# An expert gate with fewer steps and operands in PSUM, a transpose placed inside a product, and another order of work in the first, second and last pair

## What is computed

```python
y = einsum('bct,bcd->bdt', x, weights[condition])      # 64x64 per batch, one of 16
result = einsum('bnd,od->bno', y, W_base) + b_base     # 1024 -> 1024
logits = einsum('bnd,ed->bne', y, W_gate)              # 8 experts
top_p, top_i = top_k(softmax(logits), 2)
route_w = sum(one_hot(top_i) * top_p / sum(top_p))     # two experts have a weight
h  = einsum('bnd,erd->bner', y, A)                     # 8 experts x rank 16
hw = h * route_w
out = x + result + einsum('bner,eor->bno', hw, B)
```

## Time and profile before

| what | us |
|---|---|
| median of 3 runs (1004.4 to 1005.06) | 1004.57 |
| the profiled execution, whole | 1005.73 |
| its span (first to last instruction) | 1003.9 |
| TensorE matmuls busy in the span | 957.7 |
| VectorE busy | 612.8 |
| GpSimd busy | 536.2 |
| ScalarE busy | 385.5 |

### The profile page before, as it was taken

The page is one execution under the profiler, slowest core; times in us unless marked ns, Lnnn a source line. Parts: engine busy times, 40 slices in busy tenths (PEclk is TensorE's granted clock), DMA queues, the critical chain, the costliest instruction groups (busy, mean ns, idle before and its releaser), DMA issues.

```text
span 1003.9 us, 17150 instructions
## 1 busy us (share of the span) xinstructions
PE 957.7 (95%) x5462; PEld 886.1 (88%) x5462; DVE 612.8 (61%) x1396; ACT 385.5 (38%) x879; POOL 536.2 (53%) x514
## 2 busy tenths in 40 slices
PE   8759999999999999999999999999999999999997
PEld 6658998998998998998998998998998998998997
DVE  4676755556755556755556755556755556755554
ACT  6343433333433333433333433333433333433331
POOL 2366555546555546555546555556555556555550
PEclk9879999999999999999999999999999999999998
DMA  9223223322223322233322233322233322233311
GB/s 298 80 95 106 84 104 115 125 104 92 86 104 115 125 104 93 85 104 115 125 104 92 86 104 115 125 104 91 87 104 115 125 104 89 88 104 115 125 63 64
DMA packets 41450, 107.10 MB, mean 107 GB/s; under 512 B 4449, under 2 KB 8674, under 8 KB 41442
## 3 DMA queue, kind: packets, MB, share of 16 engines
...
...
## 4 chain that ended last, share of the span: by engine, by line
PE 77%; DVE 15%; issue 6%; ACT 1%; DMA 0%; POOL 0%; SPq 0%; DVEq 0%; ACTq 0%; POOLq 0%
PE ps L690 38%; PE ps_r L690 18%; PE ps_out L718 9%; PE ps_out L708 9%; DVE pick L595 5%; DVE z_sum L557 4%; DVE route L598 4%; DVE w L591 2%; PE ps L749 1%; DMA r_raw<-in_w_t 0%; ACT w_hi L401 0%; PE ps_r L749 0%; PE ps_hwt L714 0%; POOL a_lo L306 0%; PE ps L737 0%
## 5 line engine op out<-in xcount | busy, mean ns | idle before, releaser
L306 POOL TENSOR_TENSOR a_lo<-raw,a_hi 128x512 fp32r<-128x512 f32 x128 | 170.1, 1350 | 249.9 <-ACT a_hi L385 249.9
L690 PE MATMUL ps<-w_hi,s_hi 128*128 128x448 f32 x496 | 183.9, 371 | 8.9 <-DVE z_sum L557 8.9
L690 PE MATMUL ps<-w_lo,s_hi 128*128 128x448 f32 x496 | 182.6, 368 | 0.0
L690 PE MATMUL ps<-w_hi,s_lo 128*128 128x448 f32 x496 | 180.3, 363 | 0.0
L557 DVE TENSOR_TENSOR z_sum<-ps,z_sum 128x448 f32<-128x448 f32 x155 | 96.2, 621 | 119.2 <-PE ps L690 119.2
L570 DVE TENSOR_TENSOR o_sb<-ps_out,o_sb 128x448 f32<-128x448 f32 (+1 forms) x192 | 94.8, 507 | 83.3 <-PE ps_out L718 83.0
L690 PE MATMUL ps_r<-r_hi,a_lo 128*128 128x264 f32 x496 | 140.9, 284 | 0.0
L690 PE MATMUL ps_r<-r_hi,a_hi 128*128 128x264 f32 x496 | 140.9, 284 | 0.0
L690 PE MATMUL ps_r<-r_lo,a_hi 128*128 128x264 f32 x496 | 140.6, 283 | 0.0
L708 PE MATMUL ps_out<-z_hi,mix 128*128 128x448 f32 (+1 forms) x384 | 123.6, 342 | 17.7 <-ACT ps_out L413 11.9
L690 PE MATMUL ps<-w_hi,a_hi 128*128 128x448 f32 x372 | 139.1, 374 | 0.0
...
## 6 DMA issues: line engine op xcount, KB each, us to landing
raw<-in_x_t SPq DMA_DIRECT2D x128, 256.0 KB, 2.7
...
```

What stands on the lines that cost most here:

```text
L306: pool.tensor_tensor(a_lo[j][:], raw[j][:], as_f32(a_hi[j][:]), ALU.subtract).then_inc(s_a_lo[j], 1)
L690: mm = pe.matmul(bank[:, 0:w.shape[-1]], a[:, k, :], w[:, k, :], start=(opens and k == 0 and q == 0), stop=(closes and k == KH - 1 and q = ...
```

## The change

**The gate.** `exp(top0 - max)` is 1, so one exponential e = exp(top1 - top0) is enough, with the weights 1/(1+e) and e/(1+e). ScalarE takes it from `top` with a scale of -1 and a bias, so `neg_top` is gone. VectorE compares expert numbers that lie in PSUM (`ps_expert`) with the two places: `eq0` in SBUF, `ps_eq1` in PSUM. Then den = 1 + e, `ps_route` = eq1·e + eq0 in PSUM, a reciprocal, and hw = h · (1/den) · `ps_route`. The three PSUM operands lie behind the transpose in the bank `ps_hwt`. The copy of h is cut in two, each beside a wait.

```diff
-                dve.tensor_copy(h_sb[:], h).then_inc(s_h, 1)
+                dve.tensor_copy(h_sb[:, 0:ER // 2], h[:, 0:ER // 2]).then_inc(s_h, 1)
                 dve.max(top[:], logits).then_inc(s_top, 1)
                 dve.wait_ge(s_top, i + 1)
-                dve.tensor_scalar(neg_top[:], top[:, 0:1], -1.0, None, ALU.mult).then_inc(s_neg_top, 1)
+                dve.tensor_copy(h_sb[:, ER // 2:], h[:, ER // 2:]).then_inc(s_h, 1)
                 dve.max_index(top_at[:], top[:], logits).then_inc(s_top_at, 1)
                 dve.wait_ge(s_top_at, i + 1)
-                dve.tensor_copy(top_atf[:], top_at[:, 0:2]).then_inc(s_top_atf, 1)
+                for eq, j in ((eq0[:], 0), (ps_eq1, 1)):
+                    dve.tensor_tensor(eq, ps_expert, top_at[:, j:j + 1].to_broadcast([P, E]),
+                                      ALU.is_equal).then_inc(s_eq, 1)
...
-                dve.reciprocal(e_inv[:], e_sum[:]).then_inc(s_e_inv, 1)
+                dve.tensor_scalar(den[:], e[:], 1.0, None, ALU.add).then_inc(s_den, 1)
+                dve.scalar_tensor_tensor(ps_route, ps_eq1, e[:], eq0[:],
+                                         ALU.mult, ALU.add).then_inc(s_route, 1)
...
+                dve.reciprocal(e_inv[:], den[:]).then_inc(s_e_inv, 1)
...
-                dve.tensor_scalar(w2[:], e2[:], e_inv[:], None, ALU.mult).then_inc(s_w2, 1)
-                for j in range(2):
-                    dve.tensor_scalar(pick[:, j, :], expert[:], top_atf[:, j:j + 1], w2[:, j:j + 1],
-                                      ALU.is_equal, ALU.mult).then_inc(s_pick, 1)
-                dve.tensor_tensor(route[:], pick[:, 0, :], pick[:, 1, :], ALU.add).then_inc(s_route, 1)
...
-                dve.tensor_tensor(hw[:].rearrange("p (e r) -> p e r", e=E), h_sb[:].rearrange("p (e r) -> p e r", e=E),
-                                  route[:].unsqueeze(2).to_broadcast([P, E, RANK]), ALU.mult).then_inc(s_hw, 1)
+                dve.scalar_tensor_tensor(hw[:].rearrange("p (e r) -> p e r", e=E),
+                                         h_sb[:].rearrange("p (e r) -> p e r", e=E), e_inv[:],
+                                         ps_route.unsqueeze(2).to_broadcast([P, E, RANK]),
+                                         ALU.mult, ALU.mult).then_inc(s_hw, 1)
```

**The transpose.** `turn_hw` of the even tile leaves its place ahead of P3 and is issued inside it, after six of its twelve matmuls (`halfway`):

```diff
-                turn_hw(2 * p)
                 pe.wait_ge(s_s_lo[4], p)
                 pe.wait_ge(s_z_sum[1, Q], p)
-                strassen(ps_5, s2_hi, s2_lo, B22, False).then_inc(s_p[3], 1)
+                strassen(ps_5, s2_hi, s2_lo, B22, False, lambda: turn_hw(2 * p)).then_inc(s_p[3], 1)
```

```diff
-            mix_chunk(0, 0, L)
             pe.wait_ge(s_z_lo[0][R], 1)
-            first(ps_r, 1, 0, "B12").then_inc(s_p[7], 1)
-            mix_chunk(0, 0, R)
-            first(ps_5, 0, 1, "B22").then_inc(s_p[3], 1)
+            first_q(ps_r, 1, 0, "B12").then_inc(s_p[7], 1)
+            mix_chunk(0, 0, L)
+            first_q(ps_5, 0, 1, "B22").then_inc(s_p[3], 1)
+            mix_chunk(0, 0, R)
             pe.wait_ge(s_ident, 1)
-            turn_hw(0)
-            first(ps_r, 1, 1, "B22").then_inc(s_p[5], 1)
+            first_q(ps_r, 1, 1, "B22", lambda: turn_hw(0)).then_inc(s_p[5], 1)
```

In pair 31 the second `plain_r` of tile 1 goes behind lora Q, the transpose of the last tile behind that, and then mix Q, lora L, lora Q, mix R and lora R; the last tile's outputs are stored in the order L, Q, R (before Q, R, L):

```diff
             p = PAIRS - 1
+            plain_r(ps_r, 1, 1, False, True).then_inc(s_r_sum[1], 1)
+            turn_hw(2 * p + 1)
             mix_chunk(p, 1, Q)
+            pe.wait_ge(s_hwt_lo, 2 * p + 2)
+            lora(1, L)
+            lora(1, Q)
             mix_chunk(p, 1, R)
-            turn_hw(2 * p + 1)
-            pe.wait_ge(s_hwt_lo, 2 * p + 2)
-            lora(1, Q)
             lora(1, R)
-            lora(1, L)
```

367 lines of the change are left out of this document (251 added, 116 removed).

## The result

The kernel after takes **953.18 us** in the median of 4 runs (952.68 to 953.55), beside 1004.49 for the kernel before (1002.5 to 1005.06, 4 runs). The ratio is 0.9492, with a 95% interval of 0.9476 to 0.9509. The forecast was 952. The profiled execution took 952.68, its span is 950.9, and 1.78 lie around it.

A forecast was written before the change was run, and what follows sets the result against it. TensorE, busy 95% of the span, bounds the kernel, so only its waits and half clock could go. Loop 32.8, start 16.8 and end 3.5 sum to 53.1 us saved, forecast 952 us (946 to 957, chance 0.62).

The forecast's parts named there:

- The loop: Pairs 2 to 30: a faster gate of 0.9 us removes 1.13 us a pair of TensorE waiting, 32.8 us in all.
- The chain behind the transpose: From hw's transpose inside P3 to lora L: 0.07 us of room, wait counted as nothing, at most 0.25 a pair.
- Rival 3: The gate stays slow despite PSUM operands: weighing 4.9 us, 5.8 saved in the loop instead of 32.8, 979; chance 0.04.
- rival 4: Slower: GpSimd falls back, the cast of `hwt` queues behind zL's, lora comes 2.4 late, 1022; chance 0.01.
- The start: Before pair 2: 8.2 us lost instead of 25.0, pair 2 at 74.5, a gain of 16.8 (11 to 21).
- 2.8: Waits in pair 0: 0.4 for the late seed, 1.7 for hw of tile 0, 0.7 for `hwt_lo` and `b_lo`.
- 1.5: Wait of P1 of pair 1 for its low part, behind five GpSimd instructions, some lengthened: 1.5 us.
- the half clock: TensorE at 1.2 GHz after start waits, costing 2.6 and 2.9 us before; the forecast had the full clock kept.
- 3.9 (1.3, 0.9, 0.8, 0.9): Waits in pair 1: mix L for its seed 1.3, P6 for T2's low part 0.9, mix R 0.8, P7 0.9.
- The end: Last pair and tail: reordering leaves 0.7 us of wait and keeps the clock at the last matmuls, a gain of 3.5.

The follow-up runs named there:

- the run without the stall: Kernel after with GpSimd subtracting the low parts of A11 and A12 of pair 1 ahead of those of s3 and s1: 955.08 us, ratio 0.9521.

## Why the prediction was right, point by point

**The loop: right.** hw was late because of the gate; 0.83 us of weighing against 0.9, 29.01 us a pair against 29.0, 32.7 us in all against 32.8. The run with the gate alone shows it (28.99), and that with the old gate shows that nothing else of the change helps there. The forecast set all of it on operands that GpSimd can't hold up; the shorter gate would have brought 0.94 us a pair even without them, and they add 0.18.

**The chain behind the transpose: right in effect, mis-sized.** No wait was forecast, none came. The transpose has 0.28 us of room instead of 0.07; L's low part, ahead of it in VectorE's queue, has the 0.07.

**Rival 3 was mis-priced.** For a gate that stays slow I gave 979, from P3's wait alone. The run gave 1006.8. The failed step was "P3 waits 0.9 to 1.0: 0.15 to 0.25 saved a pair": it held the chain behind the transpose as on time, while it hangs on the same late VectorE, so a pair became 0.57 us longer than before. That is the mechanism of rival 4 (the casts of the transpose behind those of L), but released by a late gate and not by GpSimd.

**The start: the sum right, its terms not, so that the sum fits is luck.** Forecast 8.2 us lost, pair 2 at 74.5; measured pair 2 at 74.09, 7.8 behind the dense 66.3. In pair 0 nothing is lost where I counted 2.8: the seed is not late (the bias was cast from 26.35, I had its landing at 28.6), nor hw of tile 0 (1.7) nor `hwt_lo` (0.7), since T1 and T3 took 4.07 us together. It was GpSimd that was held up, two of its sums 2.95 and 2.16 us. So P1 of pair 1, which waits for GpSimd, stood 3.37 and not 1.5, and the half clock came back, which the forecast had excluded: from P1 to P2 5.07 us instead of the 3.40 of the run without the stall, 1.7 more. Behind that I counted 3.9 (1.3, 0.9, 0.8, 0.9) and find 0.18, about 0.4, 0.46 and 0.40, and 0.51 at lora that I hadn't foreseen. These measured terms make 7.0 of the 7.8. The table was even earlier (17.47) than the 18 to 20.5 that I had put. The step that failed was to let the contention fall on VectorE and not on both. The gain of the start isn't the order's alone either, as the forecast had it: the new gate brought 6.9 us there by itself, the new order with the old gate 12.6, both together 17.2. And the half clock behind the 3.37 us, which cost after 1.7, cost 1.2 more in another execution with the same code.

**The end: 3.1 against 3.5.** The new order brings 2.4. The forecast also counted on it to keep the clock at the last matmuls, about 1.2 us. That term isn't shown: the old order kept it in four of five traces, with either gate, and the 0.7 that are left of the 3.1 lie within the 1.1 that the one execution of before paid for its half clock (2.47 us against 1.35 to 1.37). That the gate brings little there was right: 31.75 with the new one, 31.98 and 32.05 with the old.
